# Narrow scores and maxima in column quarters, earlier second cross weights and first up weights, order places reset

## The reference

```python
def _attn(q, k, v):                      # 16 heads
    scores = jnp.einsum('bhnd,bhmd->bhnm', q, k) * HD ** (-0.5)
    p = jax.nn.softmax(scores, axis=-1)
    return jnp.einsum('bhnm,bhmd->bhnd', p, v)
x = x + attn(norm(x), norm(x)) @ Wo0 + b     # self, 1024 x 1024 scores
x = x + attn(norm(x), context) @ Wo1 + b     # cross, 1024 x 77 scores
x = x + gelu(norm(x) @ W1 + b1) @ W2 + b2    # MLP, inner width 1024
```

## Time and profile before

| | us |
|---|---|
| median of 3 runs | 4180.77 (4179.33 to 4186.44) |
| profiled execution | 4186.25 |
| its span, first to last instruction | 4184.3 |
| mean granted TensorE clock | 0.960 |
| busy: TensorE, its weight loads, VectorE, ScalarE, GpSimd | 3861.7, 2307.5, 2886.0, 2047.3, 1470.4 |
| narrow attention, layers 0 and 1 | about 20 to 651, 793 to 1350 |
| wide self, layers 2 and 3 | about 1500 to 2434, 2881 to 3771 |
| wide cross, layers 2 and 3 | about 2436 to 2745, 3773 to 4029 |
| wide MLP, layers 2 and 3 | about 2746 to 2875, 4030 to 4184 |

### The profile page before, as it was taken

One profiled execution on the slowest core, in us unless ns is written; L12 is line 12 of the kernel. 1 busy time (PEld: TensorE's weight loads), 2 busy tenths in 40 slices (PEclk: granted clock), 3 DMA queues, 4 the chain that ended last, 5 costly groups with the idle time before them and its releaser, 6 DMA issues.

```text
span 4184.3 us, 53400 instructions
## 1 busy us (share of the span) xinstructions
PE 3861.7 (92%) x19532; PEld 2307.5 (55%) x19532; DVE 2886.0 (69%) x4235; ACT 2047.3 (49%) x3724; POOL 1470.4 (35%) x842
## 2 busy tenths in 40 slices
PE   7999978899998989988999968988999999998999
PEld 5333347533334766545555446776555555546778
DVE  6889755788865677786777845545778777774465
ACT  2666655366665534443444436643444444445641
POOL 2200132220104155665566544321444444451130
PEclk7999989999998989999999989998999999999999
DMA  5233240333233333332332223342332223214320
GB/s 142 40 54 44 46 84 15 62 46 57 32 54 68 81 71 70 67 68 48 71 68 58 46 73 82 77 84 63 70 71 60 64 67 71 65 36 119 88 59 21
DMA packets 152229, 268.09 MB, mean 64 GB/s; under 512 B 33962, under 2 KB 67684, under 8 KB 151072
## 3 DMA queue, kind: packets, MB, share of 16 engines
q1 hardware_dynamic: 151968, 264.67, 30.0%
HBM read 103.96 MB, written 29.64 MB: 32 GB/s over the span
## 4 chain that ended last, share of the span: by engine, by line
PE 46%; DVE 6%; POOL 4%; issue 3%; SPq 2%; ACT 2%; DMA 1%; POOLq 0%; DVEq 0%; ACTq 0%
PE PS L1249 22%; PE PS L1430 9%; PE PS L1472 5%; PE PS L1321 4%; PE PS L1560 2%; DVE t L1991 2%; POOL t L2302 1%; PE PS L1440 1%; PE PS L1352 1%; DVE PS L2071 1%; PE PS L1364 1%; POOL t L2275 1%; SPq L2460 1%; SPq L2443 1%; POOL t L2283 1%
## 5 line engine op out<-in xcount | busy, mean ns | idle before, releaser
L1249 PE MATMUL PS<-t 128*128 128x512 f32 (+5 forms) x7896 | 1956.7, 379 | 109.1 <-DVE t L1909 16.5
L1712 ACT ACTIVATE t<-PS 128x512 f32<-128x512 f32 (+2 forms) x1600 | 1154.5, 750 | 1008.4 <-PE PS L1249 1002.4
L1249 PEld LDWEIGHTS PS<-t 128*128 128x128 f32 (+3 forms) x7896 | 1222.4, 183 | 656.4 <-issue 249.5
L1430 PE MATMUL PS<-t 128*32 128x512 f32 (+2 forms) x4352 | 815.7, 615 | 0.0
L1991 DVE TENSOR_REDUCE t<-PS 128x1 fp32r<-128x1024 f32 x512 | 618.2, 1218 | 242.0 <-PE PS L1321 240.3
L1997 DVE TENSOR_REDUCE t<-PS 128x1 f32<-128x512 f32 x1024 | 647.9, 683 | 67.4 <-PE PS L1325 64.9
L2302 POOL TENSOR_TENSOR t<-t 128x1024 f32<-128x1024 f32 x256 | 619.8, 2421 | 89.4 <-ACT t L1712 61.0
L2298 POOL TENSOR_TENSOR t<-t 128x1024 f32<-128x1024 f32 x64 | 154.1, 2407 | 698.3 <-PE PS L1440 576.2
L1325 PE MATMUL PS<-t 96*128 96x512 bf16 x1024 | 363.0, 393 | 25.8 <-DVE t L1997 15.1
L1321 PE MATMUL PS<-t 128*128 128x512 f32 x1024 | 337.8, 413 | 47.3 <-DVE t L1991 20.6
L1430 PEld LDWEIGHTS PS<-t 128*32 128x32 f32 (+2 forms) x4352 | 171.2, 122 | 332.7 <-issue 328.8
(11 more groups left out here) (134 smaller groups left out, 3491.9 us busy)
## 6 DMA issues: line engine op xcount, KB each, us to landing
t<-t SPq DMA_DIRECT2D x640, 128.0 KB, 2.6
t<-scr_n SPq DMA_DIRECT2D x288, 128.0 KB, 6.3
t<-t SPq DMA_DIRECT2D x128, 256.0 KB, 3.9
scr_n<-t SPq DMA_DIRECT2D x72, 256.0 KB, 2.4
t<-t SPq DMA_DIRECT2D x256, 64.0 KB, 2.1
t<-in_L_Wg SPq DMA_DIRECT2D x16, 768.0 KB, 4.5
t<-in_L_W SPq DMA_DIRECT2D x36, 256.0 KB, 3.4
t<-in_L_Wo SPq DMA_DIRECT2D x64, 128.0 KB, 2.5
```

The costliest lines, as they stand in the source:

```text
L1249: ins = e.matmul(out, l, r, start=i == 0, stop=i == len(terms) - 1, tile_position=tp)
L1430: ins = e.matmul(banks[S.ot][wd * j:wd * j + wd, :], u.v[j][kt], P[0:S.pr, j, :], start=kt == 0, stop=kt == S.nkt - 1, tile_position=(0, w ...
L1712: e.activation(dst, src, ACT.Exp, scale=S.L.scale).then_inc(*expd.inc((S.i, i)))
```

## The change

1. In the narrow self-attention each `max` matmul and each `score` matmul is issued as four matmuls of 32 weight columns, each to its own 32-column tile and its own 32 partitions of the same bank (`quarters`). Cross-attention scores and maxima stay as they are. What is computed is the same.
2. In the wide cross stages group 1's `w_load` goes to place -18.99 and its `w_split` to -18.3.
3. In the wide layers the first pieces of the MLP's up weights (two in layer 2, three in layer 3) are loaded from place 25.5 and split from 29.2 of the cross stage on, ahead of the barrier, into tiles that lie apart from the attention's (`up_weights`, `up_part`).
4. The table `MOVES` is reset in some 90 entries, most of them by hundredths to tenths of a place; one moves `mturn` of layer 1's first unit by 3.321 within stage 3 (layer 0's MLP).

The diff, with one stage of the table:

```diff
     3: {
+        ('down', 'mlp', 0): 0.234,
+        ('ln_turn', 0, 0, 2): 0.418,
+        ('mturn', 'self'): 3.321,
+        ('ones16', 'self', 0): 0.89,
+        ('up', 'mlp', 0): 0.033,
+        ('up', 'mlp', 1, 0, 2): -0.536,
...
@@ -630,10 +665,20 @@
                 S.Z = sbt(c, [64, 2 * CT])
                 S.T4 = [sbt(c, [128, 2 * CT]) for _ in range(4)]
 
+    def up_weights(S, c, lo, hi):
+        pair = [sbt(c, [128, 2, hi - lo], F32R)[:, :, :] for _ in range(2)]
+        S.ups = S.ups + [(lo, hi, pair)] if lo else [(lo, hi, pair)]
+
+    def up_part(S, at, wide):
+        lo, hi, pair = [u for u in S.ups if u[0] <= at < u[1]][0]
+        return [w[:, :, at - lo:at - lo + wide] for w in pair]
+
+    def down_weights(S, c):
+        S.w2h, S.w2l = [sbt(c, [128, 8, D], F32R)[:, :, :] for _ in range(2)]
+
     def mlp_weights(S, c):
-        FW = S.L.FW
-        S.w1h, S.w1l = [sbt(c, [128, 2, FW], F32R)[:, :, :] for _ in range(2)]
-        S.w2h, S.w2l = [sbt(c, [128, 8, D], F32R)[:, :, :] for _ in range(2)]
+        up_weights(S, c, 0, S.L.FW)
+        down_weights(S, c)
 
     def mlp_tiles(S, c):
         S.G = [(sbt(c, [128, 512], F32R), sbt(c, [128, 512], F32R)) for _ in range(4)]
@@ -696,8 +741,14 @@
             attention_tiles(C, c)
             if L.rope:
                 C.CS, C.roped = first.CS, first.i
+            early = M.L.FW if L.i == 3 else 512
+            if L.i == 2:
+                sbt(c, [128, 2000])
+            up_weights(M, c, 0, early)
         with ExitStack() as c:
-            mlp_weights(M, c)
+            if early < M.L.FW:
+                up_weights(M, c, early, M.L.FW)
+            down_weights(M, c)
             mlp_tiles(M, c)
             mlp_input(M, c)
             if L.i == 2:
@@ -947,6 +998,7 @@
                 if i:
                     S.chunks.append(("down", i - 1))
             S.chunks.append(("down", 3))
+            S.early = 3 if n == 8 else 2
             S.cross = [T for T in stages if T.L is S.L and T.kind == "cross"][0]
 
     for p in line:
@@ -1045,8 +1097,9 @@
                     at = 2 * pi if pi > 1 else -10
                     plan.put(at, at, [("wo", S, pi)])
                 if S.cross:
-                    plan.put(-9, -9, [("w_load", p, 1), ("qstack", S, 0), ("qstack", S, 1), ("w_split", p, 1, 1)]
-                             + nat64_steps(S, 1, 0))
+                    plan.put(-18.99, 0, [("w_load", p, 1)])
+                    plan.put(-18.3, 0, [("w_split", p, 1, 1)])
+                    plan.put(-9, -9, [("qstack", S, 0), ("qstack", S, 1)] + nat64_steps(S, 1, 0))
                     for g in range(2, 8):
                         o, pg = 4 * g - 9, S.parts[g // 4]
                         plan.put(o + (0 if L.rope else 0), 0, [("w_load", pg, g % 4)])
@@ -1059,6 +1112,10 @@
                         plan.put(2 * pi - 3.632, 0, [("qstack", S, pi)])
                     norm_put(plan, nxt, 6.75, 9.057)
                     norm_put(plan, S.parts[1].next, 23.476, 30)
+                    M = [T for T in stages if T.L is L and T.kind == "mlp"][0]
+                    for j in range(M.early):
+                        plan.put(25.5 + 0.1 * j, 0, [("m_load", M, j)])
+                        plan.put(29.2 + 0.4 * j, 0, [("m_split", M, j)])
                 else:
                     v = [("v64", S, 0, t) for t in range(2)]
                     plan.put(-9, -8, [("qstack", S, 1)] + v[0:1]
@@ -1092,6 +1149,8 @@
                     plan.put(30.5, 30.55, weight_steps(last))
         else:
             for j, (way, i) in enumerate(S.chunks if S.L.style == 64 else []):
+                if j < S.early:
+                    continue
                 plan.put(-4 + 0.1 * j, 0, [("m_load", S, j)])
                 plan.put(max(2 * (i % 4) - 2.5, -2) if way == "up" else 2 * i + -0.122, 0, [("m_split", S, j)])
             for b, p in enumerate((S.parts[1], S.parts[1].next)):
@@ -1223,10 +1282,10 @@
     def m_chunk(S, j):
 
         way, i = S.chunks[j]
-        hi, lo = (S.w1h, S.w1l) if way == "up" else (S.w2h, S.w2l)
         at = (slice(0, 2), slice(256 * i, 256 * i + 256)) if way == "up" else (slice(2 * i, 2 * i + 2), slice(0, D))
         stage = STG[:, 512 * (j % 3):512 * (j % 3) + 512].rearrange("p (k n) -> p k n", k=2)
-        return stage, hi[:, at[0], at[1]], lo[:, at[0], at[1]], at
+        hi, lo = up_part(S, 256 * i, 256) if way == "up" else [t[:, at[0], at[1]] for t in (S.w2h, S.w2l)]
+        return stage, hi, lo, at
 
     def kv_ready(w, S, i):
 
@@ -1247,6 +1306,11 @@
         def acc(out, terms, tp=None):
             for i, (l, r) in enumerate(terms):
                 ins = e.matmul(out, l, r, start=i == 0, stop=i == len(terms) - 1, tile_position=tp)
+            return ins
+
+        def quarters(out, l, r):
+            for c in range(0, 128, 32):
+                ins = e.matmul(out[c:c + 32, :], l[:, c:c + 32], r, start=True, stop=True, tile_position=(0, c))
             return ins
 
         for what, *a in order:
@@ -1322,7 +1386,7 @@
                     ins.then_inc(*bank_full[k].inc(nth))
                     continue
                 o, k, nth = take(w, ring, ("max", S.i, m, j, qt, half))
-                e.matmul(o, u.smq[j][qt], u.smk[j][half], start=True, stop=True).then_inc(*bank_full[k].inc(nth))
+                quarters(o, u.smq[j][qt], u.smk[j][half]).then_inc(*bank_full[k].inc(nth))
             elif what == "cmax":
                 S, m, j, q0 = a
                 u = S.sus[m]
@@ -1401,7 +1465,9 @@
                     w.wait_ge(expd, (S.after.i, 2 * S.after.nkt * len(S.after.units) + i - 2))
                 if S.L.style == 16:
                     for jj in range(2):
-                        ins = acc(pairs[i % 2][0:S.kr, 512 * jj:512 * jj + 512], u.st[2 * pr + jj][kt])
+                        at = pairs[i % 2][0:S.kr, 512 * jj:512 * jj + 512]
+                        (l, r), = u.st[2 * pr + jj][kt]
+                        ins = acc(at, ((l, r),)) if S.cross else quarters(at, l, r)
                 else:
                     ins = acc(banks[i % 2][0:S.kr, :], u.st[pr][kt])
                 ins.then_inc(*scored.inc((S.i, i)))
@@ -1543,7 +1609,7 @@
                 for i, gc in enumerate((m + 8, m) if S.L.i == 3 else (m,)):
                     w.wait_ge(m_low, (S.i, "up", gc // 2))
                     o, k, nth = take(w, ring, ("up", S.i, b, half, m, i))
-                    acc(o, high_low(S.w1h, S.w1l, slice(128 * gc, 128 * gc + 128), p.H,
+                    acc(o, high_low(*up_part(S, 128 * gc, 128), slice(0, 128), p.H,
                                     slice(512 * half, 512 * half + 512))).then_inc(*bank_full[k].inc(nth))
             elif what == "down":
                 S, b, half, m = a
@@ -2545,6 +2611,10 @@
                     w.wait_ge(m_low, (S.i,) + S.chunks[j - 3])
                 elif S.L.style == 16:
                     w.wait_ge(w_low_p, (S.cross.parts[0].key, 0))
+                else:
+                    w.wait_ge(w_low_v, (S.cross.parts[1].key, 3))
+                    if S.L.rope:
+                        w.wait_ge(nat_low, (S.cross.i, len(rope_order(S.cross)) - 1))
                 e.dma_start(stage, A[f"L{S.L.i}_W" + ("1" if S.chunks[j][0] == "up" else "2")][:, at[0], at[1]]
                             ).then_inc(*m_in[j % 3].inc((S.i, j), 16))
             elif what == "store":
```

57 lines of the change are left out of this document (43 added, 14 removed).

## The result

The changed kernel takes **4155.2 us** (median of four runs, 4146.8 to 4156.5) against 4180.1 us before (now the median of four): ratio 0.9934, 95% interval 0.9916 to 0.9951, so 21 to 35 us faster. The forecast was 4144 with a range of 4120 to 4170. Its profiled execution took 4155.75 us, span 4153.8. Three executions of this whole study, at mean granted clocks of 0.28 to 0.77, took 6723 to 12507 us and are left out of all that follows.

The account below looks back on a forecast made before the run. TensorE, busy 92% of the span, was taken as the bound. Terms -10 - 6.5 - 15.5 - 1.6 - 3 = -36.6 us, taken from the median of 4180.77, gave 4144 us; range 4120 to 4170.

Parts of the forecast that it names:

- -10 was forecast: Narrow self-attentions: fewer changes between full width and tiles save 14 us, of which 10 arrive; ends 0 and -14.
- the fp32 price: Narrow self-attentions: a trip into tiles and out into full-width fp32 work costs 0.34 us, against 0.23 into bf16 work.
- not all of it arrives: Narrow self-attentions: VectorE, with 351 us of work in 420, takes back some of the saving: 14 becomes 10 us.
- Rival (b): Narrow stages: VectorE becomes the bound and part 1 gives nothing, 4154 us; chance 0.22.
- What a quarter costs: Narrow self-attentions: a group of four quarter matmuls takes 0.22 us, and the extra instructions cost nothing.
- Rival (a): Narrow self-attentions: quarters are dearer than full width, 0.025 us a group, +51 us, giving 4195 us; chance 0.07.
- weight-load rule: Narrow self-attentions: quarters share rows, so each group would show a 27 ns load; part 1 55 us dearer, sum 4199.
- -6.5 forecast: Layer 2's wide cross start: earlier load and split of second weights save 6.5 us (0 to -10); layer 3 nothing.
- -15.5 forecast: Wide MLP starts of layers 2 and 3: early up weights save 16.7 us, less 1.2 for added work (-6 to -19).
- rival (c): Wide MLP starts: something else is late behind the barrier, half of part 3 stays, 4152 us; chance 0.12.
- The charge for the added work: Wide cross stages: added roundings and differences for the early up weights cost 1.2 us, charged for GpSimd.
- -4.6 forecast: Place table: -1.6 us from the moved maxima transpose in layer 0's MLP, -3 for some 90 other places.

Follow-up runs that it names:

- maxima alone: Kernel before with only the maxima matmuls of the two narrow self-attentions in quarters, scores at full width: 4222.0 us, ratio 1.0098.
- two pairs: Changed kernel against old places, compared twice, the second time on one chip: 4155.2 against 4148.8 us, then 4155.1 against 4150.8.
- The parts alone: Kernel before with only part 1, only part 2 or only part 3, one run each: 4165.7, 4175.6 and 4168.7 us.
- old places: Changed kernel with the table `MOVES` of the kernel before, so parts 1 to 3 without part 4: 4148.8 us, repeated at 4150.8.

## Why the prediction was right and wrong

The side and the range were right; the time came out 11 us above 4144, with 25 us gained of the 36.6 forecast. Some of that is luck: part 1 gave about 7 us more than it was given, and part 4 about 9 less.

**Part 1, quarters: too small.** -10 was forecast, 17 (12 to 22) measured alone. The mechanism is shown twice: by the timelines, and by the kernel with maxima alone, whose 275 more trips cost 41 us (31 to 51) where the prices said 48. In the starts a change costs 0.09 us into tiles and 0.10 to 0.14 out of them, also beside fp32 work once the 0.11 us of the earlier trace rows are taken off. The step that failed is the fp32 price: 0.34 us counted 0.11 us that four such matmuls lose whether or not the form changes. With 0.23 the working gave 23 for the 14 taken; the traces' 0.17 us a trip give 17 for its 100 trips fewer. The second step that failed is "not all of it arrives": TensorE's wait for VectorE's maxima was 5.3 us before and is 5.6 now, with VectorE at 83% of the value steps' stretch, where it was 82%. Rival (b) did not happen. What the sum left out is the start: layer 0's first value step begins at 107.93 us instead of 105.12, and in every kernel with quarters at 105.7 to 108.3 instead of 105.1 to 105.6. There the maxima stand between small full-width products, and the quarters make changes where there were none: a round of four maxima and eight such products took 3.70 us (78.59 to 82.29) and takes 3.81 (75.25 to 79.06). Whether that is all of the 2.8 us is open.

**What a quarter costs: right.** 0.22 us a group, nothing for the instructions. Rival (a) is refuted by the rows at 299.45 to 302.05. The weight-load rule of the Trainium skill ("TensorE: Matmul & The Clock Gate", section "Packing small matmuls — row/col tiling"), which would have made part 1 an estimated 55 us dearer, does not hold for these column tiles by the same rows.

**Part 2: right in size, wrong in one step.** -6.5 forecast; -6.8 in the stage, 8 (5 to 12) in the run, nothing in layer 3. The wait of TensorE was to be 4 us and is 6.7, because the subtractions took 3.9 us beside GpSimd. By the trace that cost nothing more: the next thing, the second group's rotation, was late anyway, and TensorE waits another 5.3 us for its data until 2461.97.

**Part 3: about right alone, by other terms.** -15.5 forecast, 15 (10 to 20) measured alone. The first up matmuls follow the barrier at once and at full clock, as forecast, and layer 3's MLP gave 7.9 of 8.4. Layer 2's gave 4.9 and 6.6 of 8.3 in the changed kernel's two traces: its down matmuls wait 2.0 us for the activation's products, which stand behind a table load and run at 1.7 us each beside GpSimd. That is rival (c)'s mechanism with a quarter of its price. The charge for the added work, 1.2 us on GpSimd, was about right: one wait of 1.0 us in layer 3's cross stage with the old table, and nothing in layer 2's. The rest of what that stage lost, 1.5 to 2.9 us, is not shown to be the early weights'.

**Part 4: wrong in sign.** -4.6 forecast, about +4 to +6 measured, in two pairs whose intervals overlap. TensorE's wait of 1.65 us for the transpose of the maxima is gone, but one ScalarE place costs 3.7 us and layer 1's self-attention about 2. The forecast of -3 for the places that were not looked at had no reason behind it but its bounds. It could have been read: ninety places can't be priced singly, but an instruction that is moved ahead of another on an in-order queue, and waits for a third engine, can be looked for.

**The sum.** The parts alone give 17 + 8 + 15 = 40 us, together with old places 33 (28 to 39) and 32 (24 to 41). No run separates the 7 us, but the traces speak for scatter: each part's share stands in the combined kernels as it does alone. Between the value steps it is 415.7 and 425.1 us alone against 416.3 and 424.5, in layer 2's cross stage -6.8 against -4.5 and -7.5, in the two MLPs -6.3 and -7.9 against -6.1, -4.2 and -7.9.

## What to carry to other kernels

Count changes of the array's form in program order, not matmuls in a form: each costs TensorE about 0.1 us, so work that stands between tiles is worth making in tiles if that takes no further pass, and turning half of a mixed sequence makes it slower. Look for what a moved instruction now stands ahead of on its in-order engine, not only for what it waits for. When stages are compared from single traces, take the difference in a stage that no edit touches as the error, and look at the granted clock of both: a stretch where it is full in both is the better measure.
